# bf16 in a weight transform: a casting load on another queue, one PSUM bank each for its transposes and its matmuls

## The reference

```python
xn = _layernorm(x, axis=-1)
# feed-forward part
up_gate = jnp.einsum('bsd,hd->bsh', x, W1)
up_lin = jnp.einsum('bsd,hd->bsh', x, W3)
hidden = jax.nn.silu(up_gate) * up_lin
hidden = fwht(hidden)                      # over the 8192 hidden elements, scaled by 1/sqrt(8192)
out = jnp.einsum('bsh,dh->bsd', hidden, W2)
# the layer
x = x + attention(xn, Wq, bq, Wk, bk, Wv, bv, Wo, bo) + ffn(xn, W1, W2, W3)
```

## Time and profile before

| | us |
|---|---|
| median of 3 runs | 8513.24 (8495.95 to 8943.85) |
| the profiled execution, its own time | 8526.25 |
| its span, slowest core (core 0) | 8524.6 |
| spans of the eight cores | 8407.5 to 8524.6 |
| busy: TensorE matmuls, VectorE, ScalarE, GpSimd | 5856.0, 2170.2, 1191.6, 192.4 |

### The profile page before, as it was taken

How to read it: one execution, slowest core, us unless ns; L and a number is a source line. 1 busy time by engine, 2 the same in 40 slices (tenths; PEclk the granted TensorE clock), 3 DMA queues, 4 the chain that set the end, 5 groups by cost and what they waited for, 6 DMA issues and landing times.

```text
span 8524.6 us, 64306 instructions; the slowest of 8 cores (8407.5 to 8524.6 us)
## 1 busy us (share of the span) xinstructions
PE 5856.0 (69%) x22728; PEld 2282.2 (27%) x23168; DVE 2170.2 (25%) x2784; ACT 1191.6 (14%) x1856; POOL 192.4 (2%) x270
## 2 busy tenths in 40 slices
PE   1014544446678888888877887887888759696968
PEld 0001211212111222222233333333333324242423
DVE  1003333423221111001034354345345430000000
ACT  0000000000232333333311111111111110000000
POOL 0000000000000000000000000000000000000000
PEclk6556666668565666577788998998999879898989
DMA  9997697688100000000022112212221233535353
GB/s 129 116 118 104 152 198 178 151 169 164 27 14 12 8 11 7 7 7 7 3 92 96 67 74 87 77 67 74 89 74 67 97 113 134 176 135 177 134 185 121
DMA packets 774373, 792.87 MB, mean 93 GB/s; under 512 B 638772, under 2 KB 704438, under 8 KB 749494
## 3 DMA queue, kind: packets, MB, share of 16 engines
q1 hardware_dynamic: 180950, 457.35, 15.9%
q0 software_dynamic: 65760, 197.16, 12.7%
q10 hardware_dynamic: 527360, 134.23, 7.9%
HBM read 633.49 MB, written 251.66 MB: 104 GB/s over the span
## 4 chain that ended last, share of the span: by engine, by line
PE 61%; DVE 13%; DMA 6%; another core or an unknown queue 6%; issue 5%; DVEq 3%; ACT 2%; ACTq 2%; SPq 2%; POOL 0%; POOLq 0%
PE p_po L1097 10%; PE p_pu L1001 10%; PE p_pg L975 8%; PE p_S L695 6%; PE p_pl L661 5%; PE p_pav L663 5%; PE p_po L1093 3%; DMA w1t<-s_tsp 3%; DVE s_linv L735 3%; ACTq L96 2%; PE p_heat L105 2%; DVEq L845 2%; PE p_pq L542 2%; SPq L96 2%
## 5 line engine op out<-in xcount | busy, mean ns | idle before, releaser
L1001 PE MATMUL p_pu<-s_xnall,s_w3tb 128*128 128x512 bf16 x4016 | 941.3, 391 | 368.7 <-DVE s_hst L1014 364.5
L975 PE MATMUL p_pg<-s_xnall,s_w1tb 128*128 128x512 bf16 x4000 | 914.0, 388 | 42.4 <-DMA s_w3tb<-w3t 37.3
L1097 PE MATMUL p_po<-s_hidtb,s_w2xd 128*128 128x512 bf16 x4013 | 890.1, 379 | 4.4
L727 ACT ACTIVATE s_P<-p_S 128x512 bf16<-128x512 f32 x1088 | 642.7, 597 | 937.6 <-PE p_S L695 757.6
L735 DVE RECIPROCAL s_linv<-p_pl 1x512 f32<-1x512 f32 x64 | 214.1, 3346 | 1721.2 <-PE p_pav L663 1721.2
L1001 PEld LDWEIGHTS p_pu<-s_xnall,s_w3tb 128*128 128x128 bf16 x4096 | 406.2, 100 | 893.4 <-issue 448.1
L695 PE MATMUL p_S<-s_qtl,s_k_fm 128*128 128x512 bf16 x1041 | 537.5, 516 | 105.8 <-ACT s_P L727 82.5
L327 PE MATMUL p_tp<-s_identb,s_xntm 128*128 128x128 bf16 x512 | 76.8, 305 | 766.4 <-DVE s_xntm L142 766.4
L661 PE MATMUL p_pl<-s_P,s_onescol 128*1 128x512 bf16 x1088 | 540.3, 497 | 21.5 <-ACT s_P L727 11.8
L975 PEld LDWEIGHTS p_pg<-s_xnall,s_w1tb 128*128 128x128 bf16 x4096 | 408.7, 100 | 536.2 <-issue 78.2
L663 PE MATMUL p_pav<-s_P,s_v_tm 128*128 128x512 bf16 x1044 | 534.0, 511 | 0.0
(11 more groups left out here) (95 smaller groups left out, 4519.9 us busy)
## 6 DMA issues: line engine op xcount, KB each, us to landing
s_w2xd<-w2x SPq DMA_DIRECT2D x64, 2048.0 KB, 8.7
s_wpB<-w SPq DMA_DIRECT2D x16, 4096.0 KB, 12.8
s_x<-x SPq DMA_DIRECT2D x32, 1024.0 KB, 7.5
w1b<-w POOLq DMA_DIRECT2D x1, 32768.0 KB, 355.4
w3b<-w POOLq DMA_DIRECT2D x1, 32768.0 KB, 668.5
w1t<-s_tsp ACTq DMA_DIRECT2D x32, 1024.0 KB, 6.5
w3t<-s_tsp ACTq DMA_DIRECT2D x32, 1024.0 KB, 7.3
s_w1tb<-w1t SPq DMA_DIRECT2D x64, 512.0 KB, 3.6
```

Source lines behind the costliest of these rows:

```text
L727: got = INC(st, s.activation(sb[f"P{pb}"][:], ps[f"S{sbk}"][:], AF.Exp, scale=SCALE), "ex")
L975: last = t.matmul(ps[f"pg{tsub}"][:], sb[f"w1tb{i}"][:, dc * 128:(dc + 1) * 128], sb["xnall"][:, dc * NOWN + tsub * 512: dc * NOWN + (tsub ...
L1001: last = t.matmul(ps[f"pu{tsub % 2}"][:], sb[f"w3tb{i}"][:, dc * 128:(dc + 1) * 128], sb["xnall"][:, dc * NOWN + tsub * 512: dc * NOWN + ( ...
L1097: last = t.matmul(ps[f"po{ob}"][:], sb[f"w2xd{i}"][:, hc * 128:(hc + 1) * 128], sb["hidtb"][:, hc * 512:(hc + 1) * 512], start=False, stop ...
```

## The change

Four edits.

1. wpA, wpB, pev0, pev1 and the PSUM tiles of the transposes (tpw0, ptr0, ptr1) become bf16, and the transposes use the bf16 identity.
2. The load of wpB, which now casts f32 to bf16, is issued from the GpSimd queue instead of SyncE's.
3. `part_tr` uses the single bank tpw0 (b = 0).
4. `part_h` uses a single bank of its own, pH, in place of tpw1; each of its matmuls waits for the ScalarE copy of the one before.

```diff
-        @blk.sync
-        def _(y, dc=dc):
+        @blk.gpsimd
+        def _(g, dc=dc):
             if dc >= 1:
-                W(y, st, "vv", self.v_bfly[dc - 1])
-            DMA(st, y, "wp", sb["wpB"][:], d["w2"][dc * 128:(dc + 1) * 128, :])
+                W(g, st, "vv", self.v_bfly[dc - 1])
+            DMA(st, g, "wp", sb["wpB"][:], d["w2"][dc * 128:(dc + 1) * 128, :])
...
         for grp in range(8 * half, 8 * half + 8):
-            b = grp % 2
+            b = 0
...
                     last = t.transpose(ps[f"tpw{b}"][:, q * 128:(q + 1) * 128],
                                        sb["wpB"][:, hcx * 128:(hcx + 1) * 128],
-                                       sb["identf"][:])
+                                       sb["identb"][:])
...
             @blk.tensor
-            def _(t, dc=dc, s512=s512, b=b, k=k):
+            def _(t, dc=dc, s512=s512, k=k, half=half, ex0=ex0):
                 if k == 0 and half == 0:
                     W(t, st, "vv", self.v_bfly[dc])
-                W(t, st, "mm", self.tpw_free[b])
-                m_h[k] = INC(st, t.matmul(ps[f"tpw{b}"][:], sb["h128b"][:],
+                if k >= 1:
+                    W(t, st, "ex", ex0 + k)
+                elif half == 1:
+                    W(t, st, "ex", ex0)
+                m_h[k] = INC(st, t.matmul(ps["pH"][:], sb["h128b"][:],
                                           sb["w2xb"][:, s512 * 512:(s512 + 1) * 512],
                                           start=True, stop=True), "mm")
-            self.tpw_free[b] = ("ex", ex0 + k + 1)
...
                 got = INC(st, s.activation(sb["w2xo"][:, s512 * 512:(s512 + 1) * 512],
-                                           ps[f"tpw{b}"][:], AF.Copy, scale=RSQN), "ex")
+                                           ps["pH"][:], AF.Copy, scale=RSQN), "ex")
...
                     last = t.transpose(ps[f"ptr{ob}"][:, q * 128:(q + 1) * 128],
                                        sb[f"pev{ob}"][:, q * 128:(q + 1) * 128],
-                                       sb["identf"][:])
+                                       sb["identb"][:])
...
-                                    ("wpA", (128, HID), F32), ("wpB", (128, HID), F32),
+                                    ("wpA", (128, HID), BF16), ("wpB", (128, HID), BF16),
...
-                                    ("tpw0", (128, 512), F32), ("tpw1", (128, 512), F32)]:
+                                    ("tpw0", (128, 512), BF16), ("pH", (128, 512), F32)]:
...
-                                    ("pev0", (128, 512), F32), ("pev1", (128, 512), F32),
+                                    ("pev0", (128, 512), BF16), ("pev1", (128, 512), BF16),
...
-                                    ("ptr0", (128, 512), F32), ("ptr1", (128, 512), F32)]:
+                                    ("ptr0", (128, 512), BF16), ("ptr1", (128, 512), BF16)]:
```

More of the change, by code:

```diff
@@ L861, in part_h @@
         ex0 = st.cnt["ex"]
+        hfree = [0, 0]
         for k in range(8):
             s512 = 8 * half + k
-            b = s512 % 2
             @blk.tensor
-            def _(t, dc=dc, s512=s512, b=b, k=k):
+            def _(t, dc=dc, s512=s512, k=k, half=half, ex0=ex0):
                 if k == 0 and half == 0:
                     W(t, st, "vv", self.v_bfly[dc])
-                W(t, st, "mm", self.tpw_free[b])
-                m_h[k] = INC(st, t.matmul(ps[f"tpw{b}"][:], sb["h128b"][:],
+                if k >= 1:
[3 more added lines that the diff above has]
+                m_h[k] = INC(st, t.matmul(ps["pH"][:], sb["h128b"][:],
                                           sb["w2xb"][:, s512 * 512:(s512 + 1) * 512],
                                           start=True, stop=True), "mm")
-            self.tpw_free[b] = ("ex", ex0 + k + 1)
         @blk.scalar
```

## The result

| | us |
|---|---|
| kernel before, median of 10 runs | 8707.8 (8495.95 to 8943.85) |
| changed kernel, median of 9 runs | 9070.1 (8953.12 to 9235.2) |
| ratio of the least disturbed executions, 95% interval | 1.0617 [1.0483, 1.0751] |
| profiled execution of the changed kernel, its own time | 9065.82 |
| its span, slowest core (core 5); the eight cores | 9064.3; 8759.5 to 9064.3 |

The change makes the kernel slower, as predicted; the time lies 20 us above the range of 8690 to 9050 and 212 us above the forecast. The ratio of the two medians is 9070.1 / 8707.8 = 1.0416, and the forecast stood 1.0405 over the median that it started from. Three more executions of the changed kernel are on record outside of its median: 8851.15, 8994.92 and 9139.21 us.

What follows compares the result with a forecast made beforehand. TensorE was taken to bound stage 3a, so edits count by its waits: -261 + 373 + 86 + 163 - 16 = +345 us on the profiled 8526.25, 8871, less 13.0 to the median: 8858 us, range 8690 to 9050.

Steps and rivals of the forecast that it cites:

- The sum: Closing step: adds the five parts to +345 us, sets them on the profiled execution's scale, shifts to the median, 8858 us.
- Part 3: Transposes of stage 3a with one bank: each group waits for the copy before, +86 us (60 to 130).
- Part 1: Butterfly on VectorE in bf16: 1.17 us per operation, p_pu's stall of 17.92 us shrinks to 1.61, -261 us.
- Rival B: Butterfly on VectorE no faster in bf16, because of four-dimensional views; the stall stays, 9119 us; chance 0.06.
- Part 2: wpB's casting load on POOL, queued behind the spill: TensorE waits 23.3 us sixteen times, +373 us (250 to 491).
- Rival C: wpB's load takes as long as wk's, 27.9 us, sharing DMA engines with spill and weight loads: 8976 us; chance 0.14.
- Rival A: wpB's casting load runs at the pace of bytes written, landing in 6.5 us: 8632 us; chance 0.08.
- Part 4: Hadamard matmuls with one bank: matmul and ScalarE copy in series, block of 12.56 us becomes 22.4, +163 us (138 to 190).
- The one replaces the other, so I book 0: TensorE's lower clock after the load wait, some 2.5 us, replaces that after the old butterfly stall of 17.92 us: 0 us.
- Rival D: The two single banks for transposes and Hadamard matmuls cost nothing, since something else paces them: 8609 us; chance 0.04.
- Part 5: Last stage's four transposes per output in bf16: 0.38 us instead of about 0.62, -16 us over 64 outputs.

Runs made afterwards that it cites:

- experiment 1: Changed kernel again, unedited, on another chip beside the kernel before: 9163.98 us median of 5, before 8832.38; lowest times 1.039 apart.
- experiment 9: Changed kernel and kernel before, both unedited, in turn on another chip: 9032.89 us median of 7, before 8809.88 median of 11.
- exp. 3: Kernel before with only the butterfly's tiles in bf16, wpB staying the f32 target of SyncE's load: 8696.28 us median of 6.
- exp. 4: Changed kernel with the casting load a step earlier and two banks again for transposes and Hadamard matmuls: 8520.23 us median of 6, ratio 0.9591.
- exp. 5: Changed kernel with two banks again for transposes and Hadamard matmuls, casting load still late: 8460.96 us, one run.
- Experiment 2: Changed kernel with only the casting load issued one step earlier, still on POOL: 8646.16 us median of 4.
- experiment 6: Kernel before with one bank for transposes and one for Hadamard matmuls, all f32, load on SyncE: 8939.35 us, one run.
- experiment 7: Kernel before with only the last stage's pev and ptr tiles in bf16: 8701.56 us median of 2.

## Why the prediction was right and wrong

**The step that failed** is the last one of "The sum": "It lies 13.0 us above the median of 8513.24, so I predict 8858 us". Of the 212 us between forecast and measurement, 195 are the distance of the two medians of the kernel before, 8707.8 of ten executions against the 8513.24 of three, and 17 are the change's (362 us between the medians, 345 in the sum). The sum was made against an execution whose eight cores were all at full clock (379 ns in both tiles), and I took a median of three runs, from 8495.95 to 8943.85, for a scale on which that is the usual state. It is not. The 8943.85 in the table was the sign, 430 us above the others' level and wider than every term of the sum, and the range, made of instruction costs alone, had no room for it. Of the 236 us by which stage 3b is longer on core 5 (1657.3 us against 1420.9 on core 1) some 195 are this. In the least disturbed executions of experiments 1 and 9 the changed kernel takes 8813 us, 45 below the forecast. That the ratio of the medians (1.0416) came out so near the forecast's 1.0405 is in part luck, since both medians mix executions with and without such cores: in experiment 9 it is 1.025.

**The sum itself**, step by step, in stage 3a:

| from, to | edit | measured | foretold |
|---|---|---|---|
| before, exp. 3 | butterfly in bf16 | -282 | -261 |
| exp. 3, exp. 4 | wpB, transposes and their copies in bf16, casting load on POOL, early | -30 | within Part 3 |
| exp. 4, exp. 5 | load late | +284 | +373 |
| exp. 5, changed | single banks | +367 | +249, with the row two above |
| together | | +340 | +361 |

- Part 1 is right in mechanism and size. The longest wait of p_pu is 2.0 us. Rival B (no faster) is ruled out by the 1222 ns.
- Part 2 is right in mechanism and too dear. TensorE waits 290.4 us, not 373: the load lands in 15.4 us on core 0 and 17.3 on core 5, not 20.5. Half of a wq load was the wrong neighbour, as was wk's 27.9 (Rival C), which has wv's right behind it; why a wq load, alone on its queue, took 36.0 us and more for twice the bytes, no run shows. Rival A needed under 9.7 us and is out as well; the estimates from the Trainium skill's fit (DMA: Bandwidth & Descriptors, "Anatomy of one DMA — SWDGE (gpsimd) path"), 6.8 and 11.6 us, lie below every landing of the sixteen (14.4 at least).
- Part 3: 9.65 and 10.02 us against 9.9 and 9.0. The half that I costed at full clock loses it on the way. (9.65 + 10.02 - 2 x 6.73) x 16 = 99 us, not 86.
- Part 4: the block is 23.66 us, so 11.1 x 16 = 178 us, not 163, within its bounds.
- "The one replaces the other, so I book 0" is the mis-sized step in stage 3a. The matmuls behind each of the two halves of transposes take 15.63 us instead of the 13.98 of an undisturbed step, and those behind the Hadamard block 16.43 instead of 15.78: 1.65 x 32 + 0.65 x 16 = 63 us, and only 40 of them (16 x 2.5) are the old stall's. Some 23 us were booked nowhere. Experiment 2 shows that they do not hang on the wait for the load, and experiment 4 that the second bank takes away most of the low clock behind transposes, but not all: 0.9 us stays behind one half of each chunk. Rival D (single banks free) is out by experiments 4 to 6.
- Part 5 holds for an output: 19.23 us, 15 us in all. The stage as a whole can't show it, as its waits for wod's load differ by more. The +361 in the table is the +345 of the sum without it.

The errors nearly cancel, which is luck: the load was overrated by 89 us, the banks underrated by 88 (367 - 30 = 337, against 249), the butterfly's gain underrated by 21.

How the lower clock of some cores comes about stays open. It mostly falls on a die's cores in pairs and changes between executions of one kernel on one chip; no run here steered it.

## What to carry to other kernels

Before a sum of instruction costs is put on the scale of a measured median, look at the spread of the runs and at the granted clock of each core in the profiled one: when the same kernel differs by 5% from run to run, the range must hold that, and edits are compared stage by stage on cores at equal clock. Price a PSUM bank by what it does to a chain of TensorE and its reader: with one bank they take turns, the turns cost more than the bank's own waits because the clock falls within them, and the cures that worked here are a second bank and, better, independent matmuls between two turns. A load is worth as much as its distance to its reader: issued one step earlier, the same casting load left no wait on TensorE.

## What the runs showed of the hardware

- TensorE's clock fell after short regular gaps as it did after a long one. TensorE idled 0.84 us of each 1.22 in the Hadamard block of the changed kernel, and a matmul there went from 0.38 to 0.58 us. With two banks and bf16 transposes it kept its level behind one half of the transposes (4.73 us) and lost it in the other (5.04 us, 64 matmuls behind it in 14.89). The two levels are 2.4 and 1.2 GHz (379 and 635 ns in the rows of tile p_pg), and the matmuls behind pay up to 2.4 us.
- The lower clock of whole cores is of another kind: most matmuls of a stage at 435 to 438 ns, 1.15 times 379, and 64 in a row in 16.98 us instead of 13.98, with no idle time ahead of them. The traces of the changed kernel and of experiments 3 and 7 show it. In experiment 3 it reached into stage 3a (0.80 where an undisturbed core has 0.96). The Trainium skill (TensorE: Matmul & The Clock Gate, Part 1) tells of a limit by peak current that takes a whole die to 13/16 of its clock as soon as three of its cores run dense matmuls, and holds it. The windows' 0.80 against 0.96 (a ratio of 0.83) is near that size; but here cores 4 and 5 were under it while 6 and 7 of the same die ran at 379 ns, and some executions had no such core at all, so the rule as stated does not hold for these runs.
- A load that casts 4 MB of f32 to 2 MB of bf16 on POOL's queue lands in 15.4 us, against 12.8 for the f32 load on SyncE's. Its medians on single cores lie between 15.0 and 18.3 us over the runs. By these rows such a load takes somewhat longer than a plain one of the bytes it reads; w2x<-s_w2xo, which moves the 2 MB that it writes, lands in 6.5.
